# The opening of a two-layer kernel: layer-norm statistics of a second chunk ahead of the wait for the constants, and one normalisation moved from ScalarE to VectorE

## The chip, the cores and the metric

The kernel runs on one core of one Trainium2 chip. The metric is the device time of one execution in microseconds. A core has TensorE (PE in the profile, PEld for its weight loads), VectorE (DVE), ScalarE (ACT), GpSimd (POOL) and SyncE (SP). Each runs its own list of instructions in order, and they meet through semaphores: an instruction waits until a named semaphore has reached a value.

## The reference, cut to what matters

Four blocks follow each other: a small state-space layer, a mixture of experts, a linear attention and a second mixture of experts, each as `x = x + layernorm(block(layernorm(x)))`. Only the opening of the first is touched:

```python
x = x + _layernorm(_L0_attn_ref(_layernorm(x), Wxproj, Wdt, bdt, Wxs, A_log, Wout, Dp))
# in _L0_attn_ref:
proj = einsum('bld,pd->blp', x, Wxproj)            # a 64-wide part for dt, then B_part and C_part
dt = softplus(einsum('blr,or->blo', dt_part, Wdt) + bdt)
A = -exp(A_log)
A_bar = exp(dt * A)
Bx = dt * B_part * einsum('bld,nd->bln', x, Wxs)
h_t = A_bar_t * h_(t-1) + Bx_t                     # a scan over 2048 tokens
y = (h * C_part) @ Wout.T + Dp * x
```

`x` is 2 sequences of 2048 tokens with 128 features.

## The kernel before

The 4096 tokens are cut into eight blocks of 512: chunk c (0 to 3) of sequence b (0 or 1), written (c,b) below. A block is four tiles of 128 tokens, with the tokens on the partitions. `X` holds all of it on the chip. Each engine's list is written out by hand, and its order is fixed; there is no planner.

In the opening, a block passes through these steps:

- SyncE loads it (`X<-in_x`, two loads a chunk, in order of c).
- VectorE takes mean and variance of its four tiles (`stats`, L1014 and L1019) and adds the epsilon (L1022). GpSimd raises the variances to the power -0.5 (L635). VectorE multiplies mean and factor into the shift (`x_shift`, L1036, semaphore `a_shift`). The function `first_stats(c)` issues this for both blocks of a chunk; the shift of (c,1) is issued in the midst of `first_stats(c + 1)`.
- ScalarE normalises the four tiles (L790, semaphore `a_xn`) into `xnf`, a ring that holds two chunks.
- TensorE transposes them (`turn(c)`, L1600), and ScalarE copies the result out of PSUM (L796).
- TensorE multiplies both blocks of a chunk by the projection weights `wa` (`project(c)`, L1608). So `project(c)` is the first step that has a whole chunk.
- ScalarE takes a magnitude of it (L799), and VectorE forms four parts of it (`parts(c)`: L1052, L1053, L1055, L1057; the last of them needs the magnitude).

When `parts(3)` is done, VectorE goes on with the softplus, the factors and the scan for all chunks at once (L1070 to L1085). ScalarE's logarithm and exponential (L804, L806) lie between.

ScalarE starts nine loads of small constants (`CON`, L775), among them `A_log` into `negA`, the identity, and the weights. One semaphore, `const_loaded`, counts all nine. VectorE waits for it after `first_stats(0)`: it clips `negA` (L1041), forms `diagD` (L1042), waits for ScalarE's exponential of `negA` (L780), negates it (L1044), and copies a 16-column product of two constants into `wa` (L1046, L1047) that TensorE has made (L1592). ScalarE's exponential of `negA` stands ahead of its first normalisation, and a table load (ACT_TABLE_LOAD) ahead of the exponential. TensorE waits for `wa` ahead of its first transpose.

GpSimd, after its eight powers, issues eight writes of zeros to `sum_dram` (L637).

Of the kernel before, what the change touches and what calls it, by code (L numbers as in the profile page):

```python
# [21 lines left out]
ALU = mybir.AluOpType  # L22
ACT = mybir.ActivationFunctionType
# [6 lines left out]
CH = 4  # L30
J = TB // CH
# [21 lines left out]
LEAD = 1  # L53
# [29 lines left out]
def program(nc, inp, outs):  # L83
    with ExitStack() as ctx:
# [31 lines left out]
        ones = sb("ones", [P, P])  # L116
# [20 lines left out]
        negA = sb("negA", [P, 1])  # L137
# [10 lines left out]
        xnA = xnf[:].rearrange("p u (b j d) -> p u b j d", b=NB, j=J)  # L148
# [20 lines left out]
        vex, rstdx, nmrx = (hit[:, 64 + 32 * k:96 + 32 * k].rearrange("p (c b j) -> p c b j", c=CH, b=NB) for k in range(3))  # L169
# [18 lines left out]
        cg = sb("cg", [P, 4])  # L188
# [233 lines left out]
        s_alog = sem("alog_clipped")  # L422
# [6 lines left out]
        s_wa = sem("wa_ready")  # L429
        s_ea = sem("exp_alog")  # L430
        a_var = sem("a_var")
        a_rstd = sem("a_rstd")
        a_xnmr = sem("a_shift")
        a_xn = sem("a_xn")
        a_xt_ps = sem("a_xt_in_psum")
# [26 lines left out]
        def at_least(eng, signal, n):  # L462
            if n > 0:
                eng.wait_ge(signal, LEAD + n)
# [77 lines left out]
        Xv = X[:, :, :, :].rearrange("p b c (j d) -> p c b j d", j=J)  # L542
# [228 lines left out]
        def _(act):  # L771
# [4 lines left out]

            for each in leading[2 * opening // 3:opening]:
                act.sem_inc(each, LEAD)
            act.wait_ge(s_alog, LEAD + 1)
            nc.scalar.activation(negA[:], negA[:], ACT.Exp).then_inc(s_ea, 1)  # L780
            act.wait_ge(s_fill, LEAD + 1)
            ch.begin(0, 0)

            for c in range(CH + 2):
                for b in range(NB):
                    if c < CH:
                        act.wait_ge(a_xnmr, LEAD + c * 2 + b + 1)
                        at_least(act, a_xt_ps, (c - 2) * 2 + b + 1)
                        for j in range(J):
                            last = nc.scalar.activation(xnA[:, c % 2, b, j], Xv[:, c, b, j], ACT.Identity,  # L790
                                                        bias=nmrx[:, c, b, j:j + 1], scale=rstdx[:, c, b, j:j + 1])
                        last.then_inc(a_xn, 1)
                for b in range(NB):
                    if 1 <= c <= CH:
                        act.wait_ge(a_xt_ps, LEAD + (c - 1) * 2 + b + 1)
                        nc.scalar.activation(xnTA[:, c - 1, b], bank[b][:], ACT.Copy).then_inc(a_xt, 1)  # L796
                if c >= 2:
                    act.wait_ge(a_proj, LEAD + c - 1)
                    nc.scalar.activation(az[32 * (c - 2):32 * (c - 1)], bank[PROJ[c % 2]][0:32, :], ACT.Abs,  # L799
                                         bias=bdt[:, 0:1]).then_inc(a_abs, 1)  # L800
# [207 lines left out]
        def _(dve):  # L1008
# [17 lines left out]
            def first_stats(c):  # L1026
                dve.wait_ge(s_x[c], LEAD + 32)
                for b in range(NB):
                    stats(lambda j: Xv[:, c, b, j], b, mvx[:, c, b], vex[:, c, b], a_var)
                    if c and b == 0:  # L1030
                        x_shift(c - 1, 1)
                x_shift(c, 0)

            def x_shift(c, b):
                dve.wait_ge(a_rstd, LEAD + c * 2 + b + 1)
                nc.vector.scalar_tensor_tensor(nmrx[:, c, b], mvx[:, c, b, :, 0], -1.0, rstdx[:, c, b], ALU.mult,  # L1036
                                               ALU.mult).then_inc(a_xnmr, 1)
            dve.wait_ge(s_out, LEAD + 0)
            first_stats(0)
            dve.wait_ge(s_const, LEAD + 16 * len(CON))  # L1040
            nc.vector.tensor_scalar(negA[:], negA[:], 85.0, None, ALU.min).then_inc(s_alog, 1)  # L1041
            nc.vector.tensor_scalar(diagD[:], ident[:], dp[:, 0:1], None, ALU.mult)  # L1042
            dve.wait_ge(s_ea, LEAD + 1)
            nc.vector.tensor_scalar(negA[:], negA[:], -1.0, None, ALU.mult)  # L1044
            dve.wait_ge(s_wdt, LEAD + 1)
            nc.vector.tensor_copy(wa[:, 0, 0:NS], bank[7][:, 0:NS])  # L1046
            nc.vector.tensor_copy(wa[:, 1, NS:2 * NS], bank[7][:, 0:NS]).then_inc(s_wa, 1)  # L1047
# [11 lines left out]
            def do(ins):  # L1059
                ch.mark(ins)  # L1060
                ch.wait()
            for c in range(1, CH):
                first_stats(c)
            x_shift(CH - 1, 1)
            for c in range(CH):
                parts(c)
            nc.vector.memset(carry[0:32], 0.0)
# [519 lines left out]
        def _(pe):  # L1587
# [2 lines left out]

            pe.wait_ge(s_const, LEAD + 16 * len(CON))
            nc.tensor.matmul(bank[7][:, 0:NS], wxp[:], wdt[:], start=True, stop=True).then_inc(s_wdt, 1)  # L1592
            pe.wait_ge(s_wa, LEAD + 1)

            def turn(c):
                for b in range(NB):
                    pe.wait_ge(a_xn, LEAD + c * 2 + b + 1)
                    at_least(pe, a_xt, (c - 1) * 2 + b + 1)
                    for j in range(J):
                        last = nc.tensor.transpose(bank[b][:, j * P:(j + 1) * P], xnA[:, c % 2, b, j], ident[:])  # L1600
                    last.then_inc(a_xt_ps, 1)
# [8 lines left out]
            for c in range(CH + 1):  # L1610
                if c < CH:
                    turn(c)
                if c:
                    project(c - 1)

# [457 lines left out]
```

## Time and profile before

| | |
|---|---|
| three runs | 702.16 us median (701.15 to 703.88) |
| the profiled execution | 703.21 us, of which the span of the trace is 701.4 us |
| busy share | PE 73%, DVE 60%, ACT 49%, POOL 44% |
| granted TensorE clock, mean | 0.85 of full |
| the opening, up to VectorE's first softplus step (L1070) | 37.15 us from the start |

Times in the rows count from the start of the span. A row of a timeline gives start, duration, engine, line and tiles; in square brackets is how long the engine sat idle before it and what it waited for. A row with x4 or x12 merges that many instructions that follow each other. Instructions of one engine overlap a little, so a row can start before the one ahead of it has ended.

### The profile page before, as it was taken

The page shows a single profiled execution, that of the slowest core. Times are in us where ns is not written, and L with a number is a line of the kernel's source. Part 1 is how long each engine was busy: PE and PEld are TensorE (multiplying, and loading weights), DVE is VectorE, ACT ScalarE, POOL GpSimd, SP SyncE. Part 2 cuts the span into 40 slices and gives each one's busy share as a digit, 9 for nine tenths or more (in the row PEclk, how much of TensorE's full clock was granted, in tenths as well). Part 3 has the DMA queues.
Part 4 walks back from the last instruction along what each step waited for, and adds up shares of the span by engine and source line. Part 5 has one row for each costly group of instructions (what it writes and reads, how often), then busy time and mean ns, then how long its engine had stood idle before and what let it go on. Part 6 is the DMA issues. An engine that isn't in the chain of part 4 may idle for free.

```text
span 701.4 us, 13529 instructions
## 1 busy us (share of the span) xinstructions
PE 514.5 (73%) x3846; PEld 374.3 (53%) x3847; DVE 421.7 (60%) x1761; ACT 343.0 (49%) x724; POOL 310.7 (44%) x329
## 2 busy tenths in 40 slices
PE   1759521588758157878899994169999999999924
PEld 1447110356435023434334432159999999999911
DVE  4789768654312279897246878964455455545456
ACT  3815533344323034444357662246666666666525
POOL 3514300358878433342002112036676776667444
PEclk9976855599987569888899997569999999999966
DMA  7501263112333421100001010011111111111164
GB/s 187 138 0 48 79 274 147 28 41 44 42 47 39 100 100 32 32 0 1 1 1 31 16 31 21 24 22 48 46 49 45 49 49 45 49 43 52 35 230 141
DMA packets 47287, 42.22 MB, mean 60 GB/s; under 512 B 15345, under 2 KB 41322, under 8 KB 46730
## 3 DMA queue, kind: packets, MB, share of 16 engines
q1 hardware_dynamic: 31658, 25.35, 11.3%
q0 software_dynamic: 10368, 15.82, 10.1%
q10 hardware_dynamic: 5216, 0.52, 0.5%
q8 instruction: 20, 0.33, 0.2%
q14 instruction: 25, 0.20, 0.1%
HBM read 26.23 MB, written 15.30 MB: 59 GB/s over the span
## 4 chain that ended last, share of the span: by engine, by line
PE 48%; DVE 26%; issue 10%; POOL 6%; ACT 6%; DMA 3%; ACTq 1%; DVEq 0%; POOLq 0%; SPq 0%
PE bank L1916 18%; PE banks L1937 4%; PE bank L1937 4%; POOL sum_dram L683 3%; DVE st L1284 3%; PE bank L1774 3%; PE bank L1764 2%; PE bank L1729 2%; POOL arena L667 2%; DVE mv L1289 2%; DVE st L1014 2%; ACT arena L938 1%; POOL rstd L700 1%; PE bank L1830 1%; DVE hit L1147 1%
## 5 line engine op out<-in xcount | busy, mean ns | idle before, releaser
L1916 PE MATMUL bank<-arena 128*128 128x128 f32 x1136 | 140.9, 278 | 0.4 <-ACT arena L989 0.4
L1916 PEld LDWEIGHTS bank<-arena 128*128 128x128 f32 x1136 | 134.7, 195 | 0.7 <-ACT arena L989 0.7
L700 POOL TENSOR_TENSOR rstd<-ve,mhalf 128x4 f32<-128x4 f32 x40 | 48.8, 1219 | 167.6 <-DVE ve L1292 119.4
L1546 DVE TENSOR_TENSOR arena<-arena,bank 128x512 f32<-128x512 f32 x71 | 48.8, 688 | 82.4 <-PE bank L1916 82.4
L754 POOL DMA_INDIRECT y_dram<-arena,sidx x71 | 69.9, 985 | 44.9 <-DVE arena L1551 41.3
L975 ACT ACTIVATE arena<-wgu 128x1024 f32 x71 | 74.9, 1057 | 26.8 <-PE bank L1916 26.4
L746 POOL DMA_INDIRECT arena<-x3row_dram,gidx x71 | 68.8, 969 | 36.4 <-issue 21.0
L981 ACT ACTIVATE arena<-bank 128x512 f32<-128x512 f32 x71 | 42.4, 597 | 43.0 <-PE bank L1916 43.0
L667 POOL DMA_INDIRECT arena<-x1row_dram,idx x32 | 31.3, 979 | 43.8 <-DVE idx L1244 34.3
L683 POOL DMA_INDIRECT sum_dram<-arena,idx x28 | 44.2, 1577 | 10.9 <-issue 7.9
L1265 DVE TENSOR_TENSOR arena<-arena,bank 128x256 f32<-128x256 f32 x32 | 13.5, 422 | 57.3 <-ACT arena L870 57.3
L1330 DVE TENSOR_TENSOR arena<-arena 128x1024 f32<-128x1024 f32 x32 | 39.2, 1224 | 10.4 <-ACT arena L901 10.2
L938 ACT ACTIVATE arena<-bank 128x512 f32<-128x512 f32 x64 | 33.0, 602 | 23.2 <-PE bank L1830 23.2
L1729 PE MATMUL bank<-w,arena 128*128 128x512 f32 x64 | 39.1, 698 | 0.0
L1774 PE MATMUL bank<-arena 128*17 128x153 f32 x512 | 27.8, 346 | 14.3 <-DVE arena L1332 14.2
L1937 PE MATMUL bank<-w,arena 128*128 x288 | 38.1, 275 | 0.0
L1937 PE MATMUL banks<-w,arena 128*128 x280 | 37.0, 275 | 0.0
L1937 PEld LDWEIGHTS bank<-w,arena 128*128 128x128 f32 x288 | 35.0, 192 | 0.2 <-issue 0.2
L1937 PEld LDWEIGHTS banks<-w,arena 128*128 128x128 f32 x280 | 34.1, 192 | 0.0
L1774 PEld LDWEIGHTS bank<-arena 128*17 128x17 f32 x512 | 13.3, 108 | 34.2 <-issue 21.7
L870 ACT ACTIVATE arena<-bank 128x256 f32<-128x256 f32 x32 | 12.3, 383 | 24.0 <-PE bank L1729 24.0
L883 ACT ACTIVATE xnf<-X,nmr,rstd 128x128 f32<-128x128 f32 (+1 forms) x32 | 13.2, 483 | 22.1 <-DVE nmr L1302 22.0
(370 smaller groups left out, 1077.0 us busy)
## 6 DMA issues: line engine op xcount, KB each, us to landing
wgu<-in_wgu SPq DMA_DIRECT2D x1, 4096.0 KB, 12.4
wgu<-y_dram SPq DMA_DIRECT2D x8, 512.0 KB, 7.2
X<-in_x SPq DMA_DIRECT2D x8, 256.0 KB, 6.4
sum_dram<-zero POOLq DMA_DIRECT2D x8, 256.0 KB, 4.2
x1row_dram<-row SPq DMA_DIRECT2D x8, 256.0 KB, 2.4
w<-in_w SPq DMA_DIRECT2D x1, 2048.0 KB, 17.3
acc<-sum_dram SPq DMA_DIRECT2D x8, 256.0 KB, 2.9
w<-in_wd SPq DMA_DIRECT2D x1, 2048.0 KB, 9.9
```

The costliest lines, as they stand in the source:

```text
L667: nc.gpsimd.indirect_dma_start(xg[:, n % XG], None, x1row_dram, bass.IndirectOffsetOnAxis(ap=idx[:, e, k:k + 1].bitcast(U32), axis=0)).the ...
L683: nc.gpsimd.indirect_dma_start(sum_dram, at, yw[:, n % 8], None, compute_op=ALU.add).then_inc(c_acc[k], 16)
L700: nc.gpsimd.tensor_tensor(out, ve[:, u], mhalf[:, 0:J], ALU.pow).then_inc(done, 1)
L746: nc.gpsimd.indirect_dma_start(xr[:, n.ring], None, x3row_dram, bass.IndirectOffsetOnAxis(ap=gidx1[:, n.n:n.n + 1].bitcast(U32), axis=0)). ...
L754: nc.gpsimd.indirect_dma_start(y_dram, bass.IndirectOffsetOnAxis(ap=sidx1[:, o.n:o.n + 1].bitcast(U32), axis=0), yr[:, o.ring], None).then ...
L975: nc.scalar.activation(wnow[:, k.pair], wgu[:, ds(e, 1)].rearrange("p o n -> p (o n)"), ACT.Copy).then_inc(f_w, 1)
L981: nc.scalar.activation(sgl[:, m.pair], bank[1 + m.pair][:], ACT.Silu).then_inc(f_silu, 1)
L1546: nc.vector.tensor_tensor(gl[:, m.pair], sgl[:, m.pair], bank[3 + m.pair][:], ALU.mult).then_inc(f_gated, 1)
L1729: nc.tensor.matmul(bank[2 + m.pair][:], xgT[:, m.pair], w13[:, ds(m.lap, 1)].rearrange("p o n -> p (o n)"), start=True, stop=True).then_in ...
L1774: last = nc.tensor.matmul(bank[3 + a.b][32 * q:32 * q + DH + 1, g_ * NF:(g_ + 1) * NF], vx[:, j, h, 0:DH + 1], kx[:, j, h, 0:NF], start=Fa ...
L1916: last = nc.tensor.matmul(bank[first + m.pair][:, h * P:(h + 1) * P], wnow[:, m.pair, at_:at_ + P], xrT[:, m.ring], start=True, stop=True)
L1937: last = nc.tensor.matmul(bank[5 + o.pair][:, 0:D], gl[:, o.pair, h * P:(h + 1) * P], wd[:, ds(e, 1), h].rearrange("p o n -> p (o n)"), st ...
```

## The change

Four edits, all in the opening:

1. VectorE runs `first_stats(1)` directly after `first_stats(0)`, ahead of the wait for the constants.
2. ScalarE's first instruction is an exponential of a column of ones into a scratch column, which needs no constant. The exponential of `negA` moves behind the normalisation of chunk 1, and VectorE's negation of it behind the last shift.
3. TensorE waits for `wa` ahead of its first projection, no longer ahead of its first transpose.
4. Block (3,1) is normalised by VectorE (four tensor_scalar instructions, X times factor plus shift), no longer by ScalarE. VectorE waits for that until both blocks of chunk 1 are transposed, since chunk 3 takes their place in `xnf`. Both engines count on `a_xn`, so TensorE waits for all eight blocks before it transposes either of chunk 3.

```diff
 @block.scalar
-            act.wait_ge(s_alog, LEAD + 1)
-            nc.scalar.activation(negA[:], negA[:], ACT.Exp).then_inc(s_ea, 1)
             act.wait_ge(s_fill, LEAD + 1)
+            nc.scalar.activation(cg[:, 0:1], ones[:, 0:1], ACT.Exp)
             ch.begin(0, 0)
             for c in range(CH + 2):
                 for b in range(NB):
-                    if c < CH:
+                    if c < CH and (c, b) != (CH - 1, 1):
                         act.wait_ge(a_xnmr, LEAD + c * 2 + b + 1)
...
+                if c == 1:
+                    act.wait_ge(s_alog, LEAD + 1)
+                    nc.scalar.activation(negA[:], negA[:], ACT.Exp).then_inc(s_ea, 1)
 @block.vector
             first_stats(0)
+            first_stats(1)
             dve.wait_ge(s_const, LEAD + 16 * len(CON))
             nc.vector.tensor_scalar(negA[:], negA[:], 85.0, None, ALU.min).then_inc(s_alog, 1)
             nc.vector.tensor_scalar(diagD[:], ident[:], dp[:, 0:1], None, ALU.mult)
-            dve.wait_ge(s_ea, LEAD + 1)
-            nc.vector.tensor_scalar(negA[:], negA[:], -1.0, None, ALU.mult)
             dve.wait_ge(s_wdt, LEAD + 1)
...
-            for c in range(1, CH):
+            for c in range(2, CH):
                 first_stats(c)
             x_shift(CH - 1, 1)
+            dve.wait_ge(s_ea, LEAD + 1)
+            nc.vector.tensor_scalar(negA[:], negA[:], -1.0, None, ALU.mult)
+            dve.wait_ge(a_xnmr, LEAD + 2 * CH)
+            at_least(dve, a_xt_ps, (CH - 2) * 2)
+            for j in range(J):
+                last = nc.vector.tensor_scalar(xnA[:, (CH - 1) % 2, 1, j], Xv[:, CH - 1, 1, j], rstdx[:, CH - 1, 1, j:j + 1],
+                                               nmrx[:, CH - 1, 1, j:j + 1], ALU.mult, ALU.add)
+            last.then_inc(a_xn, 1)
             for c in range(CH):
                 parts(c)
 @block.tensor
-            pe.wait_ge(s_wa, LEAD + 1)
             def turn(c):
                 for b in range(NB):
-                    pe.wait_ge(a_xn, LEAD + c * 2 + b + 1)
+                    pe.wait_ge(a_xn, LEAD + (c * 2 + b + 1 if c < CH - 1 else 2 * CH))
...
                 if c < CH:
                     turn(c)
+                if c == 1:
+                    pe.wait_ge(s_wa, LEAD + 1)
                 if c:
                     project(c - 1)
```

The orders below print the semaphore for which an instruction waits. VectorE before, from the last step of chunk 0's statistics (L1036, the shift of block (0,0)) on:

```order
L1036 SCALAR_TENSOR_TENSOR hit<-hit 128x4 [waits a_rstd]
L1041 TENSOR_SCALAR negA<-negA 128x1 [waits const_loaded]
L1042 TENSOR_SCALAR diagD<-ident,dp 128x128
L1044 TENSOR_SCALAR negA<-negA 128x1 [waits exp_alog]
L1046 COPY wa<-banks 128x16 [waits wdt_product]
L1047 COPY wa<-banks 128x16
L1012 MEMSET gate 128x1 [waits x_loaded_1]
```

VectorE of the change, from the last steps of chunk 1's statistics (L1038 in the third row is the shift of block (1,0)) on:

```order
L1021 BN_AGGR hit<-st 128x2 x4
L1024 TENSOR_SCALAR hit<-hit 128x4 [waits dve_chain]
L1038 SCALAR_TENSOR_TENSOR hit<-hit 128x4 [waits a_rstd]
L1044 TENSOR_SCALAR negA<-negA 128x1 [waits const_loaded]
L1045 TENSOR_SCALAR diagD<-ident,dp 128x128
L1047 COPY wa<-banks 128x16 [waits wdt_product]
L1048 COPY wa<-banks 128x16
L1014 MEMSET gate 128x1 [waits x_loaded_2]
```

What follows the constants is chunk 2 (`x_loaded_2`) where it was chunk 1, since all of chunk 1 now stands ahead of them; and the wait for the exponential is gone from this place.

ScalarE before, from the table load on:

```order
L780 ACT_TABLE_LOAD
L780 ACTIVATE negA<-negA 128x1 [waits alog_clipped]
L790 ACTIVATE xnf<-X,hit 128x128 [waits a_shift,constants_filled]
L790 ACTIVATE xnf<-X,hit 128x128 x3
L790 ACTIVATE xnf<-X,hit 128x128 [waits a_shift]
```

ScalarE of the change:

```order
L780 ACT_TABLE_LOAD
L780 ACTIVATE cg<-ones 128x1 [waits constants_filled]
L789 ACTIVATE xnf<-X,hit 128x128 [waits a_shift]
L789 ACTIVATE xnf<-X,hit 128x128 x3
L789 ACTIVATE xnf<-X,hit 128x128 [waits a_shift]
```

The table load stood first before too; what is gone from ahead of the first normalisation is the wait for the clipped `A_log`.

VectorE before, between the last shifts and the first part of chunk 0:

```order
L1022 TENSOR_SCALAR hit<-hit 128x4 [waits dve_chain]
L1036 SCALAR_TENSOR_TENSOR hit<-hit 128x4 [waits a_rstd] x2
L1052 COPY arena<-bank 32x512 [waits a_proj]
L1053 COPY arena<-bank 32x512
L1055 TENSOR_TENSOR arena<-arena,bank 32x512 [waits dve_chain]
```

VectorE of the change at that place:

```order
L1038 SCALAR_TENSOR_TENSOR hit<-hit 128x4 [waits a_rstd] x2
L1067 TENSOR_SCALAR negA<-negA 128x1 [waits exp_alog]
L1071 TENSOR_SCALAR xnf<-X,hit 128x128 [waits a_xt_in_psum,a_shift]
L1071 TENSOR_SCALAR xnf<-X,hit 128x128 x3
L1053 COPY arena<-bank 32x512 [waits a_proj]
```

Five instructions now stand between the last shift and the first part. The order of GpSimd and of SyncE is the same as before.

## Rows read from the trace of the kernel before

**Rows 1.** The page: the span, and shares of the chain that ended last, by engine.

```profile
span 701.4 us, 13529 instructions
PE 48%; DVE 26%; issue 10%; POOL 6%; ACT 6%; DMA 3%; ACTq 1%; DVEq 0%; POOLq 0%; SPq 0%
```

**Rows 2.** That chain in order of time, pieces from 5 to 25 us.

```profile
5.02 6.59 DMA wg<-in_wg
...
18.97 0.58 ACT arena L796
19.69 1.94 PE bank L1600 x8
21.63 2.45 PE bank L1608 x4
...
24.68 3.17 ACT xnf L790 x8
```

**Rows 3.** The timeline of ScalarE, 8 to 29 us.

```profile
8.14 1.28 ACT L780 ACT_TABLE_LOAD   x1 [7.97 <-issue]
11.82 0.20 ACT L780 ACTIVATE negA<-negA 128x1 f32<-128x1 f32 x1 [2.40 <-DVE negA L1041]
11.93 1.63 ACT L790 ACTIVATE xnf<-X,hit 128x128 f32<-128x128 f32 x4
14.34 4.72 ACT L790 ACTIVATE xnf<-X,hit 128x128 f32<-128x128 f32 x12 [0.78 <-DVE hit L1036]
...
27.76 1.05 ACT L796 ACTIVATE arena<-bank 128x512 f32<-128x512 f32 x2
```

**Rows 4.** The timeline of VectorE, 9 to 38 us.

```profile
9.71 0.15 DVE L1036 SCALAR_TENSOR_TENSOR hit<-hit 128x4 f32<-128x4 f32 x1
11.63 0.15 DVE L1041 TENSOR_SCALAR negA<-negA 128x1 f32<-128x1 f32 x1 [1.77 <-DMA wg<-in_wg]
...
12.75 0.29 DVE L1014 BATCH_NORM_STATS2 st<-X 128x6 f32<-128x128 f32 x1
...
15.71 0.29 DVE L1014 BATCH_NORM_STATS2 st<-X 128x6 f32<-128x128 f32 x1
...
22.75 0.16 DVE L1036 SCALAR_TENSOR_TENSOR hit<-hit 128x4 f32<-128x4 f32 x1 [1.06 <-POOL hit L635]
24.10 0.68 DVE L1052 COPY arena<-bank 32x512 f32<-32x512 f32 x1 [1.19 <-PE bank L1608]
...
26.98 0.68 DVE L1052 COPY arena<-banks 32x512 f32<-32x512 f32 x1
...
29.54 0.74 DVE L1057 TENSOR_SCALAR arena<-banks,bdt 32x512 f32<-32x512 f32 x1 [0.45 <-ACT arena L799]
31.33 0.69 DVE L1052 COPY arena<-bank 32x512 f32<-32x512 f32 x1 [1.05 <-PE bank L1608]
...
37.15 0.42 DVE L1070 TENSOR_SCALAR arena<-arena 128x512 f32<-128x512 f32 x1
```

**Rows 5.** Loads of X: issue to landing, of issues 2 to 4.

```profile
L553 SPq DMA_DIRECT2D X<-in_x x3: 487/499/515, 1.2 to 2.3; - x3
...
DMA to landing us min/median/max: 4.2/5.0/6.8
```

**Rows 6.** One source line: VectorE's normalisation of four tiles elsewhere in the kernel.

```profile
L1117 DVE TENSOR_SCALAR row<-X,mv,rstd x4: 341/344/346, 84.1 to 84.8; 128x128 f32<-128x128 f32 x4
```

**Rows 7.** The timeline of GpSimd, 22 to 50 us.

```profile
22.67 6.22 POOL L637 DMA_DIRECT2D sum_dram<-zero  x8
```

**Rows 8.** The timeline of TensorE, 23 to 30 us.

```profile
24.77 1.88 PE L1608 MATMUL banks<-arena,wa 128*128 128x512 f32 x4
28.47 1.10 PE L1600 MATMUL bank<-ident,xnf 128*128 128x128 f32 x8 [1.82 <-ACT arena L796]
```

**Rows 9.** Stretches: length; busy PE, PEld, DVE, ACT, POOL; granted clock; DMA share, GB/s.

```profile
20.00:21.00 1.00, 1.00 (x7) 1.00 (x6) 1.00 (x7) 1.00 (x4) 0.77 (x1) 1.00 0.49 130
...
59.00:60.00 1.00, 1.00 (x6) 1.00 (x6) 0.97 (x7) 1.00 (x4) 0.65 (x1) 0.50 0.00 0
```

## The prediction

> **What bounds the kernel now.** I read the page first, for the shares of the chain that ended last: 48% of the span is TensorE and 26% VectorE [rows 1]. Most of that lies behind the opening, which the change doesn't touch. What matters is whether the opening is on this chain, so I read the chain in order of time. It is: it begins with the load of the ninth constant (issued at 5.02, landed at 11.61), goes through ScalarE's normalisations, a copy at 18.97, TensorE's transposes and projection to 24.08, and ScalarE again [rows 2]. Then I read the timelines of ScalarE and VectorE for the waits. There are five to see:
>
> - ScalarE starts its first normalisation at 11.93, though the shift of block (0,0) was issued at 9.71 and takes 0.15 [rows 3, 4]. It was held by the exponential of `negA`, and that by the constants.
> - VectorE sat idle 1.77 us until the constants came [rows 4]. The statistics of chunk 1 began only at 12.75, so ScalarE had to wait 0.78 for the shift of block (0,1), which is issued in their midst [rows 3].
> - From 14.34 ScalarE is busy without a gap until the copies at 27.76 [rows 3].
> - VectorE waits 1.19 us for the first projection (24.10), 0.45 for ScalarE's second magnitude (29.54), and 1.05 for the third projection (31.33) [rows 4]. After 31.33 it does `parts(2)` and `parts(3)` back to back and starts the softplus at 37.15. Everything later hangs on that instruction.
> - The last shift of the eight waits 1.06 for GpSimd's power (22.75) [rows 4].
>
> So the question is how much earlier than 37.15 the instruction L1070 comes.
>
> **Edits 1 to 3: the start.** After the shift issued at 9.71 VectorE's next instruction can issue 0.08 later, at 9.79 (my estimate, as its small instructions issue elsewhere in that timeline). Is chunk 1 there? Its second load is issued at 2.3 and took 6.8 us, so 9.1 [rows 5]: yes, by 0.7 us. A chunk of statistics takes 15.71 - 12.75 = 2.96 us [rows 4], so chunk 1 ends at 12.75. By then the constants (11.61) and TensorE's small product are long there. The four instructions left between take about 0.55 (11.63 to 12.75 was 1.12 [rows 4], less some 0.43 of waits for the exponential and the product and 0.15 of the negation, which left; I round the rest). So chunk 2 starts at 13.30 and chunk 3 at 16.26.
>
> ScalarE's table load ended at 8.14 + 1.28 = 9.42 [rows 3]. It ran ahead of the wait for the constants before, too, so "table first" gains nothing; the small exponential is hidden ahead of 9.86. ScalarE then starts at 9.90. It needs (4.72 - 1.63)/8 = 0.386 us a tile [rows 3], 1.54 a block. A block (c,1) can start 1.59 after the statistics of chunk c+1 did (12.75 to 14.34 [rows 3, 4]). Hence (0,0) at 9.90, (0,1) at 11.44 (its shift allows 11.38), (1,0) at 12.99, and (1,1) not at 14.53 but at 13.30 + 1.59 = 14.89, a new wait of 0.36. ScalarE is free at 16.44. The exponential of `negA` takes 0.11 (11.82 to 11.93 [rows 3]), and the copies of chunk 0 start at 16.55 instead of 18.97 [rows 2]: **2.42 us earlier**. Nothing between them and VectorE's first part changes, so `parts(0)` can start at 24.10 - 2.42 = 21.68.
>
> **Edit 4: VectorE's four tiles.** No row of this place exists. The last shift came 4.08 after chunk 3's start (12.75 + 2 × 2.96 = 18.67 to 22.75 [rows 4]), so now at 20.34. The negation and the wait for that shift add some 0.16. The nearest price is L1117: four tiles of the same size with two per-partition operands, each 0.344, the last begun 0.7 to 0.8 after the first, 1.13 in all [rows 6]. VectorE is free at 21.63, just ahead of 21.68: the cost is nothing, because the wait for the first projection hides it. That cover has 0.05 to spare; each microsecond beyond is on the path, and without the cover the edit would cost VectorE 1.2. The wait for chunk 1's transposes is over by some 19.2 (16.55 plus 2.66, from 18.97 to 21.63 [rows 2]).
>
> Its yield is on ScalarE: after the first magnitude it has four tiles, not eight, ahead of the copies of chunk 2. These come at 27.76 [rows 3] - 2.42 - 1.54 = 23.80, and TensorE could deliver the third projection at 31.33 - 3.96 = 27.37. VectorE by itself needs 26.98 - 24.10 = 2.88 for one `parts` [rows 4]: from 21.70 it has done two at 27.46. So VectorE becomes the bound, both its waits (0.45 and 1.05) go, and `parts(2)` starts at 27.46, **3.87 us earlier** than 31.33. The fourth projection needs `parts(1)` done, also 27.46; it took 1.88 [rows 8] and is there by 29.4, ahead of `parts(3)` at 30.34. L1070 comes at 33.28.
>
> **The sum.** 2.42 from the start and 1.45 from the two waits, 3.87 in all. Against the profiled execution's own time it is 703.21 - 3.87 = 699.3; that execution is 1.05 above the median of the runs, 702.16, so by the median **698.3**. All that follows is chained to L1070, and I found no load that a step soon after it waits for.
>
> **A port that two engines share.** GpSimd's eight zero writes took 6.22 us from 22.67 on, 0.78 each [rows 7]; they start right after its last power and so now at about 20.3, beside VectorE's four tiles. L1117 ran with no such neighbour. The bound from above is one such issue that VectorE has to sit out, 0.78, all of it on the path: gain 3.1 in place of 3.87; from below it is 0, as the shift at 22.75 took 0.16 beside these writes and 0.15 without them [rows 4]. I take 0, and keep 0.78. The Trainium skill, "SBUF — State Buffer", section "SBUF: two separate sides", says that VectorE in a two-port mode and GpSimd exclude each other for a whole instruction, and calls it a trap for DMAs that GpSimd issues. By that page the sum would be 3.1 if GpSimd comes first, and 3.87 with later zero writes if VectorE does; the shift, which has two inputs on the chip, does not decide it.
>
> **The rivals.**
>
> *TensorE's clock comes up later.* The granted clock reads 1.00 at 20 to 21 us [rows 9], yet eight transposes took 1.94 at 19.69 and 1.10 at 28.47, and a projection 2.45 at 21.63 and 1.88 at 24.77 [rows 2, 8]: these are the half and the full level (1.2 and 2.4 GHz), with the change inside the first projection. The work now starts 2.4 earlier and need not take the rise along. A projection all at half is, as an estimate, 2 × 1.88 = 3.76, 1.3 more than 2.45: gain 2.6, 699.6. If the second chunk is at half too (0.84 + 1.88 more, less 0.3 of slack), the gain is near 0.2: 702. The Trainium skill, "TensorE: Matmul & The Clock Gate", section "What's actually happening", says that the throttled state is the default and that activity releases it; the transposes at 19.69 agree.
>
> *The other side: the clock stays down.* At 59 to 60 us TensorE was busy the whole microsecond at 0.50 [rows 9], so work alone doesn't bring it up at once. If it stayed at half through the opening, turn and project would take 5.7 a chunk: with the first turn from 17.3, projections end at 23.0, 28.7, 34.4 and 38.2, and `parts(3)` at 41.1, 3.9 later than now: 706. It decides from a rise after about 28.7 on; a rise before that leaves a gain. Against it: before, it had risen by 24.77.
>
> *Lost later.* Stages that are bound by TensorE see another clock at another moment. Three runs of the same kernel already differ by 2.7 us. A loss of 2 to 4 leaves 700.5 to 702.
>
> *The change doesn't do what it says.* If chunk 1 landed 0.7 later than in this trace, `first_stats(1)` would wait and push the constants' work behind it; each microsecond of that costs a microsecond of the 2.42. I fold it into the first rival.
>
> **How the numbers follow.** The forecast: 0.60, 697.3 to 699.6. Clock or port, gain 0.2 to 3.1: 0.20. Lost later: 0.10. More than 5 gained, by a luckier clock: 0.06. The other side: 0.04. The range leaves out the slower case and the ends of the others: 696.8 to 701.2. A measurement of this kernel can tell about 0.5% from no change, which is 3.5 us, and the forecast of 3.87 lies just beyond: of its 0.60 about 0.44 is beyond 698.65. With the lucky case that is 0.50 faster, 0.45 within 0.5%, and 0.05 slower.
>
> **What the profile of the changed kernel would show.** Right: the first normalisation at 9.9, no idle time on VectorE ahead of the constants' work, the copies of chunk 0 at 16.6, L1071 ending by 21.7, `parts(0)` at 21.7 and four `parts` without a gap, the softplus (L1079) at 33.3. Wrong: VectorE waiting for a load of X at 9.8; L1071 at more than 0.4 a tile; `parts(1)` waiting for a projection of more than 2.5; or the softplus at 33.3 and the end not 3.9 earlier, which would put the loss behind the opening.

## The result, and the profile after

| | before | change |
|---|---|---|
| runs beside each other | 702.39 us median (701.15 to 703.88, 4) | 696.10 us median (694.81 to 696.67, 4) |
| ratio | | 0.9907, 95% interval 0.9882 to 0.9932 |
| the profiled execution (its span) | 703.21 (701.4) | 696.60 (694.8) |
| softplus of VectorE starts | 37.15 | 34.10 |
| from there to the end of the span | 664.3 | 660.7 |
| mean granted clock | 0.85 | 0.853 |

The change gains 6.3 us, 0.9%. The forecast was 3.9, and 696.10 lies 0.7 below the range. In the traces (spans 701.4 and 694.8) the softplus comes only 3.05 us earlier; the other 3.5 us come behind it. Two executions of later kernels, 920 and 1052 us long where all others of theirs lie within 6 us, are left out below.

The timeline of ScalarE in the change, to be read against [rows 3]:

```profile
8.24 1.28 ACT L780 ACT_TABLE_LOAD   x1 [8.08 <-issue]
9.54 0.20 ACT L780 ACTIVATE cg<-ones 128x1 f32<-128x1 f32 x1
9.91 6.50 ACT L789 ACTIVATE xnf<-X,hit 128x128 f32<-128x128 f32 x16 [0.17 <-DVE hit L1038]
16.31 0.19 ACT L794 ACTIVATE negA<-negA 128x1 f32<-128x1 f32 x1
16.40 1.05 ACT L798 ACTIVATE arena<-bank 128x512 f32<-128x512 f32 x2
```

The first normalisation starts at 9.91 (forecast 9.90), sixteen tiles run as one piece, and the copies of chunk 0 start at 16.40 (forecast 16.55, before 18.97). The timeline of VectorE, against [rows 4]:

```profile
12.74 0.15 DVE L1044 TENSOR_SCALAR negA<-negA 128x1 f32<-128x1 f32 x1
...
13.17 0.29 DVE L1016 BATCH_NORM_STATS2 st<-X 128x6 f32<-128x128 f32 x1
...
20.21 0.16 DVE L1038 SCALAR_TENSOR_TENSOR hit<-hit 128x4 f32<-128x4 f32 x1 [1.06 <-POOL hit L635]
20.29 0.15 DVE L1067 TENSOR_SCALAR negA<-negA 128x1 f32<-128x1 f32 x1
20.41 1.12 DVE L1071 TENSOR_SCALAR xnf<-X,hit 128x128 f32<-128x128 f32 x4
22.51 0.68 DVE L1053 COPY arena<-bank 32x512 f32<-32x512 f32 x1 [0.98 <-PE bank L1616]
...
25.40 0.68 DVE L1053 COPY arena<-banks 32x512 f32<-32x512 f32 x1
...
28.29 0.69 DVE L1053 COPY arena<-bank 32x512 f32<-32x512 f32 x1
...
31.19 0.69 DVE L1053 COPY arena<-banks 32x512 f32<-32x512 f32 x1
...
34.10 0.42 DVE L1079 TENSOR_SCALAR arena<-arena 128x512 f32<-128x512 f32 x1
```

The row at 12.74 has no bracket: the wait for the constants costs nothing now. The four tiles take 1.12 us. Of the three waits of before only the first is left, 0.98 for the first projection; the four parts then follow each other every 2.9 us. All of this is the forecast, shifted by the one thing that is not: the first part starts at 22.51 instead of 21.7. TensorE's timeline has the reason, against [rows 2, 8]:

```profile
17.12 1.94 PE L1608 MATMUL bank<-ident,xnf 128*128 128x128 f32 x8 [2.68 <-ACT arena L798]
18.85 3.62 PE L1616 MATMUL bank<-arena,wa 128*128 128x512 f32 x4
22.27 1.23 PE L1608 MATMUL bank<-ident,xnf 128*128 128x128 f32 x8
23.33 1.88 PE L1616 MATMUL banks<-arena,wa 128*128 128x512 f32 x4
```

The first projection takes 3.62 us here, nearly twice the 1.88 of the next: it ran at 1.2 GHz to its end, and the first rise of the granted clock falls at 22.6. GpSimd's zero writes ran beside the four tiles and took as long as before [rows 7]:

```profile
20.13 6.22 POOL L637 DMA_DIRECT2D sum_dram<-zero  x8
```

Behind the softplus no instruction differs but its time does. The chain that ended last, before, 78 to 93 us:

```profile
78.93 2.85 PE bank L1643 x4
...
86.36 2.56 PE bank L1643 x4
...
92.55 0.30 DVE qi L1140
```

and the change:

```profile
75.75 3.52 PE bank L1653 x4
...
83.84 3.53 PE bank L1653 x4
...
90.98 0.30 DVE qi L1149
```

The same products take 0.7 to 1.0 longer in the change, so of 3.05 us only 1.57 are left at this point. Later it wins more back. Stretches of before (columns as in [rows 9]):

```profile
255.00:335.00 80.00, 65.19 (x626) 31.49 (x624) 69.08 (x253) 36.33 (x107) 27.40 (x36) 0.85 0.05 14
335.00:355.00 20.00, 17.16 (x88) 5.90 (x84) 3.79 (x10) 8.05 (x15) 0.00 (x0) 0.83 0.00 1
```

and of the change:

```profile
255.00:335.00 80.00, 62.13 (x639) 30.72 (x638) 66.98 (x247) 38.42 (x109) 27.35 (x36) 0.91 0.05 14
335.00:355.00 20.00, 18.43 (x109) 6.54 (x107) 5.18 (x15) 9.52 (x19) 0.00 (x0) 0.91 0.00 1
```

At 0.91 of full clock instead of 0.85 TensorE does 639 products in 62.1 us there instead of 626 in 65.2. Taken from the start of the same VectorE instruction in both traces, the change is 2.5 us ahead at 268 us, 6.1 at 354, and 6.6 at the end of the span. So two questions are open: what the opening is worth without the luck of one trace, and whether the rest comes from the edits or from where the clock happened to change.

### The profile page after: what moved, and what is told of

Its sections match the earlier page's. It is cut to its first block, busy times and chain, and to the rows that moved or that the text cites. A ratio compares the mean times of both kernels' runs of the same rounds, so it can differ in the third digit from the quotient of the medians.

```text
span 694.8 us, 13528 instructions
## 1 busy us (share of the span) xinstructions
PE 512.1 (74%) x3845; PEld 374.3 (54%) x3847; DVE 422.2 (61%) x1765; ACT 341.3 (49%) x721; POOL 310.7 (45%) x329
## 4 chain that ended last, share of the span: by engine, by line
PE 44%; DVE 29%; issue 11%; POOL 8%; ACT 4%; DMA 3%; ACTq 0%; DVEq 0%; POOLq 0%; SPq 0%
PE bank L1926 19%; PE banks L1947 5%; PE bank L1947 4%; POOL sum_dram L683 4%; DVE st L1293 4%; POOL arena L667 3%; PE bank L1784 2%; DVE mv L1298 2%; DVE st L1016 2%; PE bank L1739 2%; ACT arena L940 1%; POOL rstd L700 1%; PE bank L1774 1%; PE bank L1840 1%; DVE arena L1339 1%
## 5 line engine op out<-in xcount | busy, mean ns | idle before, releaser
L1947 PE MATMUL bank<-w,arena 128*128 x288 | 38.1, 276 | 0.0
L1784 PE MATMUL bank<-arena 128*17 128x153 f32 x512 | 26.1, 330 | 16.2 <-DVE arena L1341 16.1
```

Source lines behind the costliest of these rows:

```text
L1784: last = nc.tensor.matmul(bank[3 + a.b][32 * q:32 * q + DH + 1, g_ * NF:(g_ + 1) * NF], vx[:, j, h, 0:DH + 1], kx[:, j, h, 0:NF], start=Fa ...
L1947: last = nc.tensor.matmul(bank[5 + o.pair][:, 0:D], gl[:, o.pair, h * P:(h + 1) * P], wd[:, ds(e, 1), h].rearrange("p o n -> p (o n)"), st ...
```

## The experiments

Behind a median stand its range and the number of executions; the kernel before ran beside each on the same chip. The spread of a difference of means is given as twice its standard error.

**The two halves on the whole kernel, and the kernel before again.** e1 takes edit 4 out of the change; e2 puts it alone into the kernel before; r1 is the kernel before.

```diff
-            dve.wait_ge(a_xnmr, LEAD + 2 * CH)
...
-            last.then_inc(a_xn, 1)
...
-                    if c < CH and (c, b) != (CH - 1, 1):
+                    if c < CH:
...
-                    pe.wait_ge(a_xn, LEAD + (c * 2 + b + 1 if c < CH - 1 else 2 * CH))
+                    pe.wait_ge(a_xn, LEAD + c * 2 + b + 1)
```

This is e1 against the change; e2 is the same difference the other way round, against the kernel before.

> The change without its fourth edit: ScalarE normalises all eight blocks. Both theories expect the first part on VectorE (parts of chunk 0) at 22.5 as in the change, the copies of chunk 2 on ScalarE 1.55 us later than in the change, the two waits of VectorE (0.45 and 1.05 us) back, and the softplus at 35.5, 1.4 later than in the change. Total by PLACE: between 696 and 702, not necessarily 1.4 above the change. By a theory EDITS (the later gain belongs to edit 4, by something that it leaves behind, such as another load on the engines or another layout of the code): 700.5, the full later gain gone. If each microsecond of the opening counts once and nothing else happens: 697.5.

> The kernel before with the fourth edit alone. The last shift still comes at 22.75, the four tiles take 1.12 as in the change and end at about 24.05, just ahead of the first projection (24.10), so that they cost nothing; the copies of chunk 2 come at 26.2 instead of 27.76, VectorE runs its four parts nearly without a gap from 24.10, and the softplus starts at 35.7 (1.4 earlier than 37.15). Total: 700.8 if each microsecond counts once; EDITS (the later gain belongs to edit 4) 697.5; PLACE: anywhere from 697 to 702.

> The kernel before, unchanged, for a second trace. In the two traces that there are, the change begins the softplus 3.05 us earlier (37.15 to 34.10) and ends 6.6 us earlier (span 701.4 to 694.8); about 3.5 us of that arise behind the opening, at places where the granted clock of TensorE stood at its other level. Theory PLACE (the clock rises and falls at the same moments in each execution of a kernel, so a shift of the opening moves the work against them): the rises and falls of this trace lie within 0.5 us of those of the first (up at 22.9, down at 43.4, up at 63.9, up at 142.4, down at 343.8, up at 350.6), and the span is within 1 us of 701.4. Theory CHANCE (they lie anywhere, and the later 3.5 us are luck of one trace): they lie elsewhere, and the span differs by some us.

Measured: e1 700.05 us (697.14 to 702.94, 10) and e2 699.01 (697.44 to 702.95, 9) beside 703.25 (25): 0.9958 (0.9930 to 0.9986) and 0.9962 (0.9934 to 0.9990). Either half gains some 3 us in the mean, and the intervals are wider than the gains. The softplus starts at 35.13 and 36.60 (35.5 and 35.7 expected). The totals don't tell the theories apart, since PLACE allowed nearly all of them.

r1 took 701.47, with the softplus at 37.96. Its clock rises at 24.6, 41.6 and 65.5 us where the first trace has 22.9 and 63.9, and its span is 1.7 us shorter, as CHANCE expected. The first projection took 3.43 us there, and in r3, a third trace of the kernel before, 3.60 (softplus at 38.12). The same row of the first trace is the lucky one of the three (the 2.45 of [rows 2] is the part of it that the chain holds):

```profile
21.42 2.64 PE L1608 MATMUL bank<-arena,wa 128*128 128x512 f32 x4
```

TensorE's timeline in r3:

```profile
21.42 3.60 PE L1608 MATMUL bank<-arena,wa 128*128 128x512 f32 x4
24.84 1.06 PE L1600 MATMUL bank<-ident,xnf 128*128 128x128 f32 x8
```

> The kernel before once more, for its trace. In the two traces of the change, TensorE's clock rises 26.1 us behind the softplus's start (34.10 to 60.2) and the rest takes 660.7; in the four others it is 26.8 (rest 664.3), 27.5 (661.7), 29.1 and 29.2 (660.8 and 661.5). Theory CHANCE: the rest hangs on these moments alone and not on the kernel, so a trace of before whose rise lies at 26.1 or 29.1 has a rest below 661.6, and one at 26.8 has 664. Theory EDITS: before has more than 661.5 at each of them.

The rise in r3 came 27.7 us behind the softplus, and the rest took 663.9. That is none of the moments for which CHANCE had named a time, so r3 decides nothing between the two.

**The opening by itself.** Four kernels end after the opening (VectorE's first product behind the scan is its last) and write `X` to the output; all later work is left out. With it goes most of the spread, so that tenths can be measured. Line numbers there, and in t5 to t8, are 10 to 20 higher. t1 is the opening of before, t2 of the change, t3 has edits 1 to 3, t4 edit 4 alone.

```diff
+            return
...
+            sp.wait_ge(a_hc, LEAD + 1)
...
+                sp.dma_start(out_s[g_], x_s[:, g_]).then_inc(s_out, 16)
+            return
```

> The kernel before, cut off after the product of scan and C part (L1085): it then stores X and ends, and leaves out all that follows. Its time is the opening's, with a constant on top, so that executions can be compared in number without what the later stages add. The first traces show the product's end at 45.7 before, 42.7 in the change. Theory LATER (the gain of the opening is what the traces show, 3 to 4 us, and the rest of the 6 arises behind it): this kernel is 3 to 4 us above the cut change. Theory OPENING (the first trace of before was a lucky one, in which TensorE's clock came up early, and on average the opening alone gives 5 to 6): 5 to 6 above, with a spread of some us from one execution to the next.

> The change, cut off at the same place. LATER: 3 to 4 us below the cut kernel before. OPENING: 5 to 6 below, and with a narrower spread, since the gap of TensorE ahead of chunk 3's transposes (1.82 us before, 0.1 in the change) is gone, in which the clock's rise can be put off.

> The change without the normalisation on VectorE, cut off at the same place. LATER: 2.4 below the cut kernel before (the shift of the copies of chunk 0 and nothing else). OPENING: also 2.4 to 3, with the wide spread of before.

> The kernel before with the normalisation on VectorE alone, cut off at the same place. LATER: 1.45 below the cut kernel before. OPENING: 3 below, with the narrow spread of the change.

| | median us | transposes behind the first copies start | first projection | softplus starts |
|---|---|---|---|---|
| t1 | 58.15 (57.81 to 58.17, 4) | 19.70 | 3.62 | 38.14 |
| t3 | 54.85 (54.59 to 55.37, 4) | 17.12 | 3.08 | 35.03 |
| t4 | 56.27 (56.18 to 56.42, 4) | 19.69 | 3.20 | 36.26 |
| t2 | 53.70 (53.54 to 53.87, 4) | 17.13 | 3.42 | 33.91 |

The opening gains 4.45 us, between the 3 to 4 of LATER and the 5 to 6 of OPENING, and the spread is tenths, where OPENING expected some us. Edits 1 to 3 give 3.30 of it, and edit 4 on top 1.15. The traces split it: the start 19.70 - 17.12 = 2.58; the projection 3.62 - 3.08 = 0.54, clock alone; then edit 4, 35.03 - 33.91 = 1.12, in which the projection took 0.34 longer, so 1.46 by itself. Edit 4 alone (t4) says the same: 38.14 - 36.26 = 1.88, of which 0.42 is the projection and 1.46 the edit. From t1 to t2 that is 2.57, 0.20 and 1.46, together 4.23, the way from 38.14 to 33.91. The timeline of VectorE in t1:

```profile
25.09 0.68 DVE L1065 COPY arena<-bank 32x512 f32<-32x512 f32 x1 [2.17 <-PE bank L1622]
...
30.54 0.74 DVE L1070 TENSOR_SCALAR arena<-banks,bdt 32x512 f32<-32x512 f32 x1 [0.46 <-ACT arena L811]
32.33 0.69 DVE L1065 COPY arena<-bank 32x512 f32<-32x512 f32 x1 [1.05 <-PE bank L1622]
```

0.46 and 1.05 are the 1.45 of the forecast; they are gone in t2 and t4, and both are there in t3.

**TensorE kept busy.** If the late clock costs something, products that do nothing should bring it up in time. `keep_up(n)` multiplies ones into an unused bank.

```diff
+            def keep_up(n):
+                for _ in range(n):
+                    nc.tensor.matmul(bank[6][:, 0:P], ones[:], ones[:], start=True, stop=True)
```

t5 (opening of before) and t6 (of the change) have seven of them ahead of the wait for the constants, and more ahead of blocks (0,1) and (1,0). t7 (before) has two, three and five ahead of blocks (0,0), (0,1) and (1,0), t8 (change) six ahead of (1,0); v2 and v1 are the same on the whole kernels.

> The cut kernel before, with 15 more products of ones on TensorE in its idle time ahead of chunk 1's transposes, so that its clock can be up before the first projection. The theory that the clock costs the opening about 1.5 us by the half-rate first projection (3.62 us in the cut kernel's trace, 1.88 at full rate) expects the first projection at 1.9 to 2.5, VectorE's first part at 23.2 to 23.6 in place of 25.09, and a time of 56.4 in place of 58.15. A theory that the first projection waits for something else (its weights, or the copies) leaves it at 3.4 and the time at 58.1.

> The cut change with 13 such products. By the clock theory the first projection takes 1.9 to 2.5 and ends at about 20.6, but VectorE is busy with its four tiles until 21.53: the first part starts at 21.6 in place of 22.32, and the time is 53.0 in place of 53.70. The gain over the cut kernel before with TensorE kept busy is then 3.4, less than 4.45, since VectorE's four tiles have lost their cover. By the other theory both stay, and so does 4.45.

Measured: 60.21 (59.87 to 60.23, 6) and 56.27 (56.15 to 56.28, 5), both 2 us and more above the kernels without. My products stood ahead of the one that `wa` waits for. TensorE's timeline in t5:

```profile
11.96 3.20 PE L1607 MATMUL banks<-ones 128*128 128x128 f32 x14 [11.96 <-issue]
15.09 0.39 PE L1611 MATMUL banks<-wdt,wxp 64*128 64x16 f32 x2
```

and VectorE's:

```profile
15.52 0.18 DVE L1059 COPY wa<-banks 128x16 f32<-128x16 f32 x1 [4.05 <-PE banks L1611]
```

The first products need only `ones`, and still begin at 11.96. VectorE waited 4.05 us for the small product, and `wa` was copied 2.94 us later than in t1 (12.58), which is more than the 2.06 lost. So the pair says nothing on the sum, though the first projection did take 1.88 in both. t7 and t8 put the products behind it; a wait for `ones` now stands ahead of the small product, which starts at 12.12 there instead of 11.96.

> The cut kernel before, with 10 products of ones on TensorE that now stand behind the product for wa (2 ahead of block (0,0), 3 ahead of (0,1), 5 ahead of (1,0)), where they hold up nobody; in the run before they stood ahead of it, and VectorE waited 4 us for it. Theory CLOCK: TensorE's clock is up before the first projection (about 21.5), which takes 1.9 in place of 3.6; VectorE's first part starts at 23.4 in place of 25.09; time 56.4 in place of 58.15. If only the late start matters and not the clock: 58.1.

> The cut change with 6 such products ahead of block (1,0), in the 2.7 us in which TensorE is idle. CLOCK: first projection 1.9, done at 20.8; VectorE's four tiles end at 21.53 and now bound the start: first part at 21.6 in place of 22.32, time 53.0 in place of 53.7; the softplus at 33.3, the moment that was forecast. The difference to the cut kernel before, kept busy likewise, is 3.4. Otherwise 53.7.

> The whole change with the same 6 products: a version that could beat both kernels. CLOCK and each microsecond counted once: 0.7 below the change, 695.6 on the chip where that was 696.4, a ratio of 0.991 to the kernel before. If what comes behind the opening hangs on when the opening ends against the rises and falls of TensorE's clock: anywhere from 694 to 699.

Measured: t7 57.15 (57.07 to 57.33, 4), t8 53.49 (53.46 to 53.51, 4), v1 697.41 (694.66 to 698.62, 6) beside 701.92 (10), 0.9941 (0.9920 to 0.9961). The first projection takes 1.88 in both cut kernels, as CLOCK expected; the times are 0.75, 0.5 and 1.8 us longer than it expected (56.4, 53.0 and 695.6). TensorE in t7:

```profile
20.78 1.88 PE L1628 MATMUL bank<-arena,wa 128*128 128x512 f32 x4
```

and in t8:

```profile
18.07 1.88 PE L1636 MATMUL bank<-arena,wa 128*128 128x512 f32 x4
```

With the clock up in time the two openings differ by 3.66 (3.4 expected). The early clock is worth 58.15 - 57.15 = 1.00 to the kernel before (then ScalarE's copies bound it, softplus at 37.14) and only 0.21 to the change, since the projection in t8 is done at 19.95 and VectorE's four tiles, begun at 20.41, aren't. There edit 4 has lost its cover, and that is why the openings are nearer to each other with the clock up. The four tiles took 1.45 us in t8 and 1.12 in v1; 0.33 of the 0.5 us by which t8 is too long is that. In v1 as well VectorE goes from the tiles to its parts without a gap, and the softplus starts at 33.15 (forecast 33.28):

```profile
20.42 1.12 DVE L1071 TENSOR_SCALAR xnf<-X,hit 128x128 f32<-128x128 f32 x4
21.57 0.68 DVE L1053 COPY arena<-bank 32x512 f32<-32x512 f32 x1
...
33.15 0.42 DVE L1079 TENSOR_SCALAR arena<-arena 128x512 f32<-128x512 f32 x1
```

v1 beats the kernel before, but not, by these numbers, the change.

**The change begun later.** If the gain behind the opening belongs to the moment at which the clock changes, the change moved in time should lose it. Fourteen or twenty idle statistics stand ahead of `first_stats(0)`.

```diff
+            dve.wait_ge(s_x[0], LEAD + 32)
+            for k in range(14):        # d4: 20
+                nc.vector.bn_stats(eq[:, 6 * k:6 * k + 6], Xv[:, 0, 0, k % J])
             first_stats(0)
```

> The change, with 14 more statistics instructions on VectorE ahead of its first ones (each 0.218 us in a row of such instructions, so about 3.05 us; they write to a scratch tile). The whole opening moves by that, and the softplus starts at 37.15, where it started before the change. PLACE: with the opening ending when it ended before, the later stages meet the clock as before, and the total is that of the kernel before, 702.2 (701.4 to 703), 6 us more than the change for 3 us of delay. EDITS (something in the changed code helps later): the later 3.5 us stay, 699.1.

> The change with 20 statistics instructions ahead (14 of them moved the softplus by 2.70 us, from 34.10 to 36.80, so 20 move it by about 3.9, to 38.0; the cut kernel before has it at 38.1). CHANCE: its time is that of the kernel before, ratio 0.999 to 1.002. EDITS: 1.5 to 2 us below, 0.9975.

Measured: d3 699.83 (697.74 to 701.00, 10), 0.9959 (0.9939 to 0.9978); d4 700.84 (698.27 to 703.40, 11), 0.9967 (0.9949 to 0.9986). The softplus starts at 36.80 and, with a first projection of 2.45 us, at 37.01. Neither time is the one that PLACE (702.2) or CHANCE (0.999 to 1.002) had named; both lie near that of EDITS (699.1 and 0.9975). The openings alone should give some 1.3 and 0.2 us (my estimate: the transposes behind the first copies start at 19.85 and 20.99, before at 19.70, and edit 4 is worth 1.46), but the means lie 3.1 and 2.2 us below the kernel before, give or take 1.0 and 1.2.

Against EDITS stands one trace: d4 holds all four edits and takes 664.0 us from the softplus to its end; r3, the kernel before, takes 663.9. So with all the edits the rest can be as long as before. That it is so on average this trace doesn't show, since it is of one of d4's longer executions (702.82).

**Both kernels once more.**

> The change, unchanged, for more executions beside the kernel before on one chip. The cut kernels differ by 4.45 us (58.15 to 53.70), the whole ones by 6.3 (2.4 by chance or not: 4 executions each). Theory CHANCE (behind the opening both kernels are the same, and each execution meets the clock at other moments): the ratio tends to 0.9937, 4.45 us below before. Theory EDITS (something of the change helps behind the opening): it stays at 0.991, 6 us below.

> The change as it is, timed once more. Theory CHANCE: the gain beyond 4.45 us, which the cut openings measured, is a draw of the clock's moments and the ratio falls nearer to 0.9937 (4.45 of 703.2). Theory SYSTEMATIC: the change gains 6 us, ratio 0.9915 or lower, with the whole interval below 0.9937. If its trace has the rise at 26.0 to 26.4 after the softplus a third time, the stretch behind it takes 660.5 to 660.8.

> The whole kernel before, with two, three and five small products of ones into an unused bank ahead of blocks (0,0), (0,1) and (1,0) of TensorE's transposes. On the cut kernel these let the first projection run at full rate (1.88 us) and the softplus start at 37.15. So that start is expected at 37.1 to 37.2. What follows rests on when TensorE's clock next rises, and the products move that moment for a kernel of before. Theory MOMENT: the stretch behind the softplus depends only on how long after the softplus the clock rises (near 60 to 66 us): 26.0 to 26.4 after it gives 660 to 661.5 us of rest, and 26.8 or more gives 663.5 or more, whichever kernel it is. Theory EDITS: the kernel before takes at least 663.5 at either moment. If the rise falls elsewhere again, nothing is told apart. The median is then 697.5 to 699 by MOMENT with a rise at 26.0 to 26.4, and 701 to 702.5 by EDITS.

Measured: r2 696.41 (695.59 to 700.14, 6) beside 703.23 (17), 0.9921 (0.9895 to 0.9947). r4 697.86 (696.35 to 699.12, 6) beside 702.03 (17), 0.9946 (0.9927 to 0.9965). r2's interval holds both 0.9937 and 0.991; r4 fits CHANCE and not SYSTEMATIC, which wanted the whole interval below 0.9937. v2 702.66 (699.42 to 706.16, 11), 1.0013 (0.9991 to 1.0035): its opening is as short as in t7 (softplus at 37.13), and nothing of that is seen at the end. Its clock rose 26.8 us behind the softplus and the rest took 663.0, half a microsecond less than either theory allowed there.

The three timings of the change give differences of means of 6.5, 5.9 and 4.2 us. Weighted by their 4, 6 and 6 executions this is 5.4, with 0.8 to either side. Of it 4.45 is the opening; 1.0, give or take 0.8, is more than that.

r4 looks unlike the first trace of the change:

```profile
37.00:75.00 38.00, 28.18 (x127) 21.21 (x128) 33.83 (x214) 15.19 (x34) 14.13 (x14) 0.66 0.13 37
...
255.00:335.00 80.00, 64.19 (x632) 30.69 (x632) 66.71 (x243) 37.44 (x107) 27.38 (x36) 0.87 0.05 14
335.00:355.00 20.00, 18.62 (x106) 6.70 (x106) 5.21 (x15) 8.28 (x16) 0.00 (x0) 0.83 0.00 1
```

The clock is 0.66 where it was 0.72, and 0.87 and 0.83 where it was 0.91. From softplus to end, in all traces of whole kernels (the rise is the first one after 55 us, in us behind the softplus):

| trace | rise | softplus to end |
|---|---|---|
| before | 26.8 | 664.3 |
| r1, before | 27.5 | 661.7 |
| r3, before | 27.7 | 663.9 |
| v2, before with busy TensorE | 26.8 | 663.0 |
| e1, edits 1 to 3 | 27.3 | 663.5 |
| e2, edit 4 | 29.1 | 660.8 |
| the change | 26.1 | 660.7 |
| r2, change | 26.1 | 660.6 |
| r4, change | 29.0 | 663.4 |
| v1, change with busy TensorE | 26.3 | 659.7 |
| d3, change later | 29.2 | 661.5 |
| d4, change still later | 27.8 | 664.0 |

The same work takes 659.7 to 664.3. The change alone covers 660.6 to 663.4, and the kernel before 661.7 to 664.3. Up to r3 the table looked as if the moment of that one rise decided the rest. r4 ends that: at 29.0 it took 663.4, where e2 at 29.1 took 660.8. The two run alike to 268 us and part by 0.7 us by 330 and by 1.7 by 478. So the moment of one rise doesn't decide it. That the later ones do is argued, not tried.

**At equal clock.** Each execution of the timings behind the first lists its mean granted clock, and this bears on what was left open. Within the executions of one kernel on one chip, 0.001 more of clock goes with 0.31 us less (a straight line fitted to all of them, which is not an experiment). The clock was 0.846 in the mean for the kernel before beside r2, 0.851 for r2, and near 0.849 for r4, v1 and the kernel before beside them. Compared at equal clock, each kernel is below the kernel before by this much:

| | measured, means | at equal clock | what the opening should give |
|---|---|---|---|
| r2, change | 5.9 | 4.2 | 4.45 |
| r4, change | 4.2 | 4.15 | 4.45 |
| v1 | 4.8 | 4.6 | 4.66 (t1 to t8) |
| e1, edits 1 to 3 | 3.0 | 3.1 | 3.30 |
| e2, edit 4 | 3.0 | 2.3 | 1.88 |
| d3 | 3.1 | 1.9 | 1.3 |
| d4 | 2.2 | 0.8 | 0.2 |
| v2 | -0.8 | -0.5 | 1.00 |

The third column is good to 0.7 to 1.0 us. All but v2 agree with the opening. So what was gained beyond it went along with a higher clock, which doesn't say what made the clock higher in d3 and d4. v2 contradicts: its shorter opening is not in its total at equal clock either, and why was not tried.

## Why the prediction was off

**Right, by the trace:** the first normalisation at 9.9; no wait for the constants; chunk 2 at 13.17 (forecast 13.30); the copies at 16.40; the last shift at 20.21 (20.34); the four tiles hidden by the wait for the first projection, with 0.98 to spare where 0.05 was forecast (that was luck: the late clock gave the cover, and in v1 there was none); 0.45 and 1.05 gone; four parts without a gap. The start measured 2.58 (forecast 2.42) and edit 4 1.46 (1.45): 4.04 against 3.87.

**The port.** The four tiles took 1.12 us beside eight zero writes that took 6.22, as before. A wait for one such write would have been 0.78. The Trainium skill, "SBUF — State Buffer", section "SBUF: two separate sides", would have cost the sum that much if GpSimd came first; this trace shows neither engine held by the other. In the cut kernels t2, t4, t6 and t8 the tiles took 1.45, beside writes that took 6.13 in t2. The extra 0.33 was hidden in t2 and t4, where VectorE still waited 0.45 and 0.27 afterwards. What it is was not tried, so a smaller cost of the neighbour isn't excluded.

**The first step that failed** is "Nothing between them and VectorE's first part changes". It took 5.13 us from the copies to the first part from one trace, in which the clock came up early (2.64 for the projection, by the timeline). Two more traces of before had 3.43 and 3.60, and t1 3.62. The same step was 6.11 long in the change. It errs twice: the change's softplus was 0.82 later than forecast (34.10 to 33.28), and the usual softplus of before is not 37.15 but near 38.1. The mechanism, the rival that the clock comes up later, was seen; its price of 1.3 was 0.98, since a projection all at half takes 3.62 and not 3.76. But the clock comes up late before, too, so it mostly cancels. Like against like, the softplus goes from 37.13 (v2) to 33.15 (v1) with the clock up in time, and from 38.12 (r3) to 34.10 without: 4.0 each way. The medians of the cut kernels say 4.45, 0.6 above the sum (with the clock up 3.66, since the tiles took 1.45 there and on the path).

**The second**, and by its size the one that put the result outside the range, is "All that follows is chained to L1070". The sum gave the stretch behind the opening nothing, and the rival beside it, "Lost later", "A loss of 2 to 4", let the clock there only take. It gave 3.5 us in the first traces, and 4.6 us lie between the shortest and the longest such stretch above. The spread was there to be seen in the 2.7 us of three runs; I put it on one side only, left 0.06 for more than 5 gained, and so ended the range at 696.8.

**What stays open.** Of the first result's 6.3 us, 4.45 is shown to be the opening. Two more timings gave less than the first, and r4 shows the change with a long remainder, so part of the rest was a draw. Whether the last 1.0 (0.2 to 1.8) is one too isn't settled: no trace of the kernel before came below 661.7 behind the softplus, and three of the four with the whole change undelayed did. d3 and d4, which also hold edit 4, gained some 2 us more than their openings give. At equal clock most of this is gone, so it goes along with TensorE's clock; whether the edits bring the higher clock about or chance does is open. v2, meant to bring the kernel before to the change's moment, came out at 26.8 again, the moment of its first trace.

## What to carry to other kernels

Where an engine's clock changes inside the stretch that is priced, take the price from several traces of the kernel before, or cut the kernel off behind the stretch and time that: four executions each told 0.2 us apart there, and sixteen of the whole kernel left 0.8 to either side. Compare the granted clock of both sides as well: beside r2 the kernel before had 0.005 less than the change, and this goes with some 1.6 us of the 5.9 that were measured. An in-order engine that waits for the last of nine loads should first be given all the work whose data is there; that was worth 2.6 us of 4 here. And where TensorE bounds the rest and its clock wanders, let the range reach by the spread of the runs to both sides of the sum.

## What the runs showed of the hardware that was not expected

- TensorE's first product starts at 11.96 to 12.12 in every trace, also in t5, where it needs only `ones`, though the constants had reached VectorE at 10.90. The profile named the load of `wg` as its releaser in some kernels and "issue" in others. What holds it was not tried; ahead of it stands a long list of semaphore increments.
- The rises and falls of TensorE's clock fall at other moments in executions of one kernel: the first rise at 22.9, 24.6 and 24.9 in three traces of before, 22.6, 22.6 and 21.9 in three of the change. The granted clock reads 1.00 ahead of it (the products ahead of it run at half rate: eight transposes take 1.94 us, and 1.10 behind it). The Trainium skill, "TensorE: Matmul & The Clock Gate", section "What's actually happening", has the throttled state as the default that activity releases; t7 and t8 agree, where ten and six products of ones brought the first rise to 15.9 and 16.6 (18.5 in v1).
- A delay of 2.7 us at the very start (softplus at 36.80 instead of 34.10) moved the median by 2.0 to 3.7 us, by which timing of the change one takes. That holds 2.7, so these runs can't say whether a microsecond at the start counts for one at the end; v2, whose opening is 1.0 shorter and whose mean is 0.8 longer (give or take 1.4), suggests that it need not.
